# Expert results of a graph and mixture-of-experts layer stored from SyncE's queue instead of ScalarE's

## The reference, cut to what matters

```python
xn = layernorm(x)                                     # 6250 rows of 256
agg = segment_sum(xn[src] * edge_weight[:, None], dst)   # 106250 edges
x = x + agg @ gnn_weight + linear_attention(xn, Wqkv, Wout, bout)
y = layernorm(x)
top_v, top_i = top_k(y @ gate_w + gate_b, 2)          # 16 experts
w = softmax(top_v)
h = relu(y @ w1[e] + b1[e])                           # 256 -> 512, for the 2 experts e of a row
expert_out = h @ w2[e] + b2[e]                        # 512 -> 256
x = x + layernorm(y + sum(w * expert_out)) * gamma + beta
```

## Time and profile before

| | us |
|---|---|
| median of three runs (2071.03 to 2091.99) | 2082.3 |
| the profiled execution, its own time | 2090.88 |
| its span, first to last instruction | 2089.2 |
| TensorE busy | 1203.9 (58%) |
| GpSimd busy | 1001.8 (48%) |
| VectorE busy | 639.7 (31%) |
| ScalarE busy | 427.5 (20%) |
| mean granted TensorE clock | 0.788 |

### The profile page before, as it was taken

The page is one execution under the profiler, slowest core; times in us unless marked ns, Lnnn a source line. Parts: engine busy times, 40 slices in busy tenths (PEclk is TensorE's granted clock), DMA queues, the critical chain, the costliest instruction groups (busy, mean ns, idle before and its releaser), DMA issues. The chain is left out here.

```text
span 2089.2 us, 23935 instructions
## 1 busy us (share of the span) xinstructions
PE 1203.9 (58%) x6790; PEld 898.3 (43%) x6790; DVE 639.7 (31%) x2282; ACT 427.5 (20%) x1141; POOL 1001.8 (48%) x1090
## 2 busy tenths in 40 slices
PE   0288898965534757531567427622677666538870
PEld 0144454444423656420455326412565555437760
DVE  7144343433422111221212401222022311424457
ACT  3033332311211212100112112110222121212330
POOL 2746666653545244667244643565244552252324
PEclk9899999987656888765688758755788787768995
DMA  9354554321224656333565346333666564159994
GB/s 326 93 182 158 174 179 153 90 82 57 69 94 153 199 175 197 102 90 99 170 193 195 96 151 224 119 92 108 209 209 210 187 221 158 36 186 308 335 331 119
DMA packets 159242, 340.85 MB, mean 163 GB/s; under 512 B 25248, under 2 KB 97952, under 8 KB 158976
## 3 DMA queue, kind: packets, MB, share of 16 engines
q1 hardware_dynamic: 69952, 165.89, 23.9%
q0 software_dynamic: 49296, 134.68, 21.1%
q10 hardware_dynamic: 39856, 38.67, 5.5%
HBM read 274.78 MB, written 64.36 MB: 162 GB/s over the span
## 5 line engine op out<-in xcount | busy, mean ns | idle before, releaser
L798 POOL DMA_INDIRECT ring<-normed_rows,src_sb x831 | 796.5, 959 | 831.0 <-PE ps L1399 502.4
L1531 PE MATMUL ps<-room 128*128 128x128 f32 x1888 | 290.8, 319 | 145.4 <-issue 117.3
L1531 PEld LDWEIGHTS ps<-room 128*128 128x128 f32 x1888 | 275.9, 232 | 156.8 <-issue 153.8
L1544 PE MATMUL ps<-room 128*128 128x256 f32 x944 | 260.9, 426 | 55.2 <-issue 50.4
L1416 PE MATMUL ps<-ident,X 128*128 128x128 f32 x294 | 75.9, 346 | 283.2 <-ACT X L869 131.6
L1330 DVE TENSOR_TENSOR desk<-ps,room 128x256 f32<-128x256 f32 x121 | 51.3, 425 | 609.8 <-PE ps L1544 349.7
L1544 PEld LDWEIGHTS ps<-room 128*128 128x128 f32 x944 | 195.3, 218 | 88.2 <-issue 55.9
L1426 PE MATMUL ps<-room,tT 128*128 128x512 f32 x392 | 194.9, 638 | 11.6 <-issue 10.9
L910 ACT ACTIVATE room<-ps,room 128x128 f32<-128x128 f32 x472 | 134.6, 369 | 311.4 <-remote 169.9
L1416 PEld LDWEIGHTS ps<-ident,X 128*128 128x128 f32 x294 | 36.7, 165 | 330.1 <-ACT X L869 153.7
L1399 PE MATMUL ps<-ring,S 128*32 128x256 f32 x1680 | 139.0, 433 | 60.9 <-issue 39.3
(11 more groups left out here) (203 smaller groups left out, 1271.0 us busy)
## 6 DMA issues: line engine op xcount, KB each, us to landing
room<-in_w2b SPq DMA_DIRECT2D x107, 640.0 KB
room<-in_w1b SPq DMA_DIRECT2D x107, 514.0 KB
room<-rows_by_slot SPq DMA_DIRECT2D x121, 128.0 KB
results_by_slot<-desk ACTq DMA_DIRECT2D x121, 128.0 KB
rows_by_slot<-desk ACTq DMA_DIRECT2D x6, 2432.0 KB
ring<-normed_rows,src_sb POOLq DMA_INDIRECT x831
normed_rows<-X SPq DMA_DIRECT2D x7, 896.0 KB, 8.2
result<-ring SPq DMA_DIRECT2D x49, 128.0 KB
```

The lines of the kernel that those rows point to most:

```text
L798: pool.indirect_dma_start(out=ring[:, b % 2 * BT + m, :], out_offset=None, in_=table, in_offset=bass.IndirectOffsetOnAxis(ap=src_sb[:, b * ...
L1531: mm = pe.matmul(hps[:, f * TS:(f + 1) * TS], w1_sb[g % WB][:, k * F + f * P:k * F + (f + 1) * P], xgT[g % 2][:, k, :], start=(k == 0), st ...
L1544: mm = pe.matmul(ops, hT[g % 2][:, f, :], w2_sb[g % WB][:, f * D:(f + 1) * D], start=(f == 0), stop=(f == FC - 1))
```

## The change

`store_y` goes from ScalarE's stream to SP's, with the register load of the tile's number. On SP it stands behind the two loads of the same step. In a run that is left out, SP now does the counting up of `ys_out` that ScalarE did.

```diff
@@ SP
                 load_rows(r, j + 3)
                 load_weights(r, j + 2)
+                if j:
+                    store_y(r, j - 1)
+                if j + 1 == RUNS[r][2]:
+                    store_y(r, j)
+
+            def store_y(r, j):
+                g, p = RUNS[r][1] + j, SUB_PART[RUNS[r][0]]
+                t = sp.value_load(ttab[0:1, g:g + 1], min_val=0, max_val=NTILES[p] + 1)
+                sp.wait_ge(y_done, g + 1)
+                sp.dma_start(ys_tiles[p][bass.ds(t, 1)].rearrange("a p d -> (a p) d"), yo[g % 2]).then_inc(ys_out[g % 2], 16)
 
             def left_out(r):
                 _, g0, n, _ = RUNS[r]
+                for i in range(2):
+                    skip(sp, ys_out[i], left_in(i, 2, 0, g0), left_in(i, 2, g0, n), 16)
@@ ScalarE
-            def store_y(r, j):
-                g, p = RUNS[r][1] + j, SUB_PART[RUNS[r][0]]
-                t = act.value_load(ttab[0:1, g:g + 1], min_val=0, max_val=NTILES[p] + 1)
-                act.wait_ge(y_done, g + 1)
-                act.dma_start(ys_tiles[p][bass.ds(t, 1)].rearrange("a p d -> (a p) d"), yo[g % 2]).then_inc(ys_out[g % 2], 16)
...
                 where_taken(act, r, j, relu, relu_done)
-                if j:
-                    store_y(r, j - 1)
-                if j + 1 == n:
-                    store_y(r, j)
 
             def left_out(r):
...
-                for i in range(2):
-                    skip(act, ys_out[i], left_in(i, 2, 0, g0), left_in(i, 2, g0, n), 16)
```

## The result

| | before | after |
|---|---|---|
| median, us | 2077.5 (4 runs, 2071.0 to 2092.0) | 2109.0 (4 runs, 2097.5 to 2116.1) |
| ratio | | 1.0152, 95% interval 1.0113 to 1.0191 |
| span of the profiled execution | 2089.2 | 2109.5 |
| mean granted TensorE clock | 0.788 | 0.783 |

The change costs 31.6 us (the ratio times the median of before; 23 to 40 by the interval). Forecast was +22, 2104 us.

What follows compares the result with a forecast made beforehand. No engine fills the span: TensorE's chain sets the pace, GpSimd following; SP and TensorE are about equally loaded in the last stage. 11 + 2 + 3 + 10 - 4 = +22 us on 2082.3 gives 2104; range over all 2080 to 2136.

Steps and rivals of the forecast that it cites:

- its own case: Whole kernel: the summed terms give +22 us, 2104, with a range of 2094 to 2118; chance 0.45.
- SP's added step in the last stage: Last 19 second weights: load, wait and DMA add 1.09 us a visit on SP; 9 us taken.
- the joins: Visits 7/8 and 100/101: SP awaits the last result before the next run's loads; layer 1 5.5 and 5.7 us later, together 11.
- The ten visits before it: Visits before the last 19 second weights: SP's added step costs 1 us.
- SP in full: Third rival: 1.09 us for each of 33 visits from 1845 on, 36; with joins +52 us, 2134; chance 0.13.
- The relief of ScalarE: Gates and copies: ScalarE loses load, wait and DMA, gates come forward about 0.9 us; -4 us, between 0 and -29.
- The left-out run: Visits 84 to 86: SP also waits for the last stores to land; 2 us, between 0 and 4.
- the starts of three further runs: Layer 1 waits for weights at three further run starts, 1.1 us each: 3 us.
- The stores' place in the queue: SP's DMA queue: stores stand behind second weights, begin some 1.3 us later, VectorE's buffer is in time; costed at nothing.
- the fourth rival: Store late behind the weights, VectorE waits for its buffer: adds 20 to 60 us to the sum, 2125 to 2165; chance 0.06.
- Hidden: First rival: SP's store steps go into its waits and the DMA queue takes up late issues; +6 us, 2088; chance 0.28.
- faster: Second rival: ScalarE's wait was the hidden bound, TensorE gets copies' and gates' time back; -23 us, 2059; chance 0.08.

Runs made afterwards that it cites:

- The kernels with one and with two loads: Kernel before plus, on SP, the tile number's load and the wait, without the DMA: 1.0086, +13 us; with that load made twice: 1.0126, +26 us.
- the kernels with one join each: Kernel before plus SP's wait for a run's last result: at visits 100/101 1.0049, +7.6 us; at visits 7/8 1.0029, +4.5 us.

## Why the prediction was right, and where it was not

**The sign, the place and the mechanism were right.** The forecast (2104, and 2094 to 2118 for its own case) put the loss on SP's added step in the last stage and on the joins. The kernels with one and with two loads show the step by itself, the kernel with the change in the last run alone shows the place, and the kernels with one join each show the joins, the last one clearly and the first just clear of nothing. The total lies 10 us above the forecast, and 22 is just under its interval of 23 to 40. Most of the gap is the last run of visits, 18 us where 9 were put.

**The joins: right mechanism, too small.** Forecast were 5.5 and 5.7 us; layer 1 came later by 7.9 and 9.1. The issue times were met: first weights forecast 1.9 us behind the result, measured 1.93; rows 3.8, measured 3.81. The term that was too small is the one after, from the issue of the rows to layer 1. The forecast let them land, be transposed and copied from 716.4 to "719 to 720", 3.1 us to its start of layer 1 at 719.5, beside first weights at 718.8. At the first join it took 5.5. The transposes began 3.7 us behind the issue (718.86 to 722.61), and before layer 1 TensorE transposes the rows of two visits with ScalarE's copy between, 1.7 us more (722.61 to 724.32). 3.8 + 3.7 + 1.7 = 9.2 is what was measured at the first, 9.27. At the last join the forecast reckoned from first weights alone; there the parts are 4.1, 4.7 and 1.7 us, 10.5 together. Timed alone the first join costs 4.5 us (0.5 to 8.6) of the 8.1 in its trace. If it does not count in full, which the interval leaves open, two errors cancelled here.

**SP's step in the last stage: the size was a guess between 0 and 23, and it lies in the upper half.** The working gave 5.9 us a visit in place of 5.34, or 10 us. The trace of the changed kernel has 5.84, and its last run is 9.3 us longer. Timed alone, that run costs 18 us (11 to 24), and the trace of that kernel has it 12.6 us longer than before. Part of it is a term that the sum lacked: the row stores' own instructions got longer, by 2.4 us in all in the trace of the result (8.5 to 10.9 us for 18) and by more on a quick chip (below). The ten visits before it were costed at 1 us; from the first transposes of visit 91 to the result of visit 100 the traces have 76.7 us before (1845.1 to 1921.9) and 76.1 after (1847.1 to 1923.2), nothing. On a quick chip it is 51.4 us before and 56.9 after, where two kernels that are unchanged in these steps have 51.5 and 53.7.

**SP in full**, the rival with 1.09 us a visit, holds on the quick chips for the last run: visits grew by 1.16 us. (Its sum of +52 leaves out the 4 us of ScalarE's relief.) At 4.82 us a visit SP's longer step shows at its full price, at 5.27 at half to two thirds. I take it that what decides is how much faster everything else is than SP; no run varies that alone.

**The relief of ScalarE: borne out.** -4 forecast, -6.4 (-10.6 to -2.3) measured on the quick chip by the kernel that gives the most part of this relief alone; what it is worth inside the change no run shows. The gate came forward by 1.0 us where 0.9 was reckoned, at the bound that the prediction had set. The copies brought nothing: TensorE's wait for them is 19.5 us, after 19.8.

**The left-out run: 2 us forecast.** From the result of visit 83 to that of visit 90 the slow chip has 47.5 us before and 46.8 after, the quick one 37.8 and 41.6. The kernel with the first join's wait, which changes nothing there, has 41.3 on a quick chip, so the 3.8 us more are no larger than what two traces differ by, and the term is not shown. The 3 us at the starts of three further runs are too small to be seen in any run here.

**The stores' place in the queue: right at nothing.** VectorE waited once for 1.6 us for its own store, as before, and on a quick chip 5.2 us after the change against 9.8 before it, so the fourth rival is out. A store was also not 0.5 us behind the second weights, as the prediction's list of signs had it, but 1.3 to 1.5: the load, moves and check come first. The step was costed with that time (1.09 us); only the sign was put wrongly.

**Hidden and faster** are out: +32 measured against +6 and -23. The Trainium skill states on its page DMA: Bandwidth & Descriptors, section Issuing engines are not separate DMA queues, that the time to initiate a DMA is usually small relative to the DMA itself. This case's traces agree with the words, and not with the first rival, which the prediction built on them. Of the 1.13 us that a step adds, the DMA instruction takes 0.37, which is small beside the 4.3 us from first weights to layer 1 of the earlier trace rows. But the whole 1.13 us recurs at every visit of 4.82 on a sequencer that has no air, and +26 us come from loads, their moves and a wait with no DMA added.

**The signs named beforehand.** SP's steps without row stores were to take 4.8 us in place of 3.7: 4.9. TensorE's waits for first weights from 1845 to 2040 were to go over 20 us: 22.1. The stage was to be 15 us longer: 19.5, from 193.2 (1845.1 to 2038.3) to 212.7 (1847.1 to 2059.8). ScalarE's waits for L1330 are gone. Layer 1 at the joins was to come some 7 us behind the result: 9.3 and 10.5.

## What to carry to other kernels

Before an instruction is moved to a sequencer that "only issues", count what that sequencer does per step of the loop, register loads and moves too, and set it against the step's time in the stage where nothing else is slack; an added register load with its wait and without any DMA cost 0.47 of its 0.57 us per visit here. A wait at the end of a loop's run takes away the prefetch across the boundary, and its price is the whole chain behind the wait (rows issued, landed, transposed, copied), not the landing of the transfer that is issued first. Compare timed kernels for a few us, since two profiled executions of the same code can be 15 us apart.

## What was not expected of the hardware

A DMA instruction on SP is not of one length. The 18 row stores in the last run had a median of 384 ns before and 665 ns in the changed kernel, where they stand directly behind the store of a result (both on quick chips). Together they took 8.5 and 14.7 us, which is 0.34 us more a visit on the engine that is the bound. First before, then after:

```profile
L713 SPq DMA_DIRECT2D result<-ring x18: 348/384/966, 1408.4 to 1487.0; - x18
```

```profile
L725 SPq DMA_DIRECT2D result<-ring x18: 433/665/1754, 1436.8 to 1532.6; - x18
```

In the kernel with the load and wait but no store on SP they stay at 394 ns, so the growth comes with the store ahead of them. Why it does stays open. These 6 us are an effect of the DMA itself, beside the instructions ahead of it, and the only one that a trace here shows.

In the last run of the changed kernel TensorE needs more busy time for the same products: 82.63 us for 529 before and 89.04 us for 528 after, with a mean granted clock of 0.98 and 0.93 between the two levels of 1.2 and 2.4 GHz (quick chips). It stands still for weights in between, and comes back at the lower clock: behind a wait of 3.08 us for first weights, which ended at 1439.75, the granted clock from 1440.5 to 1443.7 was 0.50, the lower level. Here SP was the bound, so how much of the 21 us this run lost is due to it cannot be told from these runs.

```profile
1403.50:1505.00 101.50, 82.63 (x529) 72.13 (x526) 54.63 (x161) 32.25 (x110) 34.94 (x36) 0.98 0.93 344
```

```profile
1428.80:1551.00 122.20, 89.04 (x528) 78.07 (x526) 53.64 (x160) 32.26 (x111) 35.25 (x36) 0.93 0.86 283
```

And chips of one kind run this kernel a third apart (1561 and 2083 us), nearly all of it where GpSimd's gathers run. The gather instruction itself is no longer (962 and 959 ns on average); GpSimd's wait for TensorE to be through with a batch is 66 us on the one and 502 us on the other. Why the chips differ stays open; the slowed instructions of SP and ScalarE's waits for "remote" above are what the traces show of it. A change of a per cent can have its place and size from this: the step cost its full 1.1 us a visit on the quick chips and half to two thirds of it (0.57 and 0.71) on the slow ones.
